# The 64-wide attention stage with its q, k, v and score products as three products of float16 parts

## The reference, cut to what matters

```
b, n, _ = x.shape                       # x is layer-normalised before
q = einsum('bnd,ed->bne', x, Wq).reshape(b, n, H, DH).transpose(0, 2, 1, 3)   # the same for k, v
q = _l2norm(q) * q_scale                # per head, over its 64 channels
k = _l2norm(k) * k_scale
attn = softmax(einsum('bhid,bhjd->bhij', q, k) * DH ** (-0.5))
out = einsum('bhij,bhjd->bhid', attn, v).transpose(0, 2, 1, 3).reshape(b, n, H * DH)
return einsum('bne,de->bnd', out, Wo) + bo
```

## Time and profile before

| | |
|---|---|
| median of 3 runs | 5605.33 us (5605.23 to 5605.4) |
| profiled execution, span | 5817.8 us, 93955 instructions; no other time of it is given |
| busy over the span | PE 4867.1 us (84%), DVE 3629.7 (62%), ACT 3333.5 (57%), POOL 1360.1 (23%) |
| mean granted clock of TensorE | 0.916 |
| this stage, within the span | 3660 to 5435 us |

### The profile page before, as it was taken

One profiled execution on the slowest core, in us unless ns is written; L12 is line 12 of the kernel. 1 busy time (PEld: TensorE's weight loads), 2 busy tenths in 40 slices (PEclk: granted clock), 3 DMA queues, 4 the chain that ended last, 5 costly groups with the idle time before them and its releaser, 6 DMA issues. The chain is left out here.

```text
span 5817.8 us, 93955 instructions
## 1 busy us (share of the span) xinstructions
PE 4867.1 (84%) x29648; PEld 2462.7 (42%) x29648; DVE 3629.7 (62%) x7303; ACT 3333.5 (57%) x5317; POOL 1360.1 (23%) x1406
## 2 busy tenths in 40 slices
PE   6999768559989967868888659799999999999578
PEld 2222268524444436842222246344344344344255
DVE  5344453477777775347777761576776776776750
ACT  6999644425555544447888722555665665655422
POOL 1111045424334405532323045000000000000055
PEclk8999879869999988989999876899999999999777
DMA  3222121213333312132323232200000000000222
GB/s 83 65 65 63 42 56 39 62 57 91 87 94 91 88 49 60 40 92 51 66 50 66 56 67 43 48 1 0 0 0 0 0 0 0 0 0 0 70 43 40
DMA packets 228016, 265.41 MB, mean 46 GB/s; under 512 B 36874, under 2 KB 194410, under 8 KB 221352
## 3 DMA queue, kind: packets, MB, share of 16 engines
q1 hardware_dynamic: 184180, 194.46, 12.6%
q0 software_dynamic: 43520, 66.97, 6.4%
HBM read 163.86 MB, written 96.65 MB: 45 GB/s over the span
## 5 line engine op out<-in xcount | busy, mean ns | idle before, releaser
L3968 ACT ACTIVATE prob_wide<-slot_wide 128x1024 f32<-128x1024 f32 x512 | 497.2, 1026 | 181.9 <-PE slot_wide L3856 181.9
L2184 ACT ACTIVATE prob_decay<-slot_decay 128x640 f32<-128x640 f32 x512 | 358.8, 705 | 343.8 <-PE slot_decay L2031 342.5
L1000 ACT ACTIVATE prob_rms<-slot_rms 128x1024 f32<-128x1024 f32 x512 | 503.9, 1090 | 56.5 <-PE slot_rms L834 54.0
L2518 DVE TENSOR_TENSOR slot_decay<-slot_decay,dtab_decay 128x512 f32<-128x512 f32 (+3 forms) x1024 | 454.1, 494 | 130.0 <-PE slot_decay L2010 109.9
L1000 ACT ACTIVATE prob_relative<-slot_relative 128x1024 f32<-128x1024 f32 x512 | 497.8, 1049 | 42.1 <-PE slot_relative L834 40.6
L3856 PE MATMUL slot_wide<-qT_wide,kT_wide 64*128 64x512 f32 x2048 | 509.5, 616 | 8.0 <-ACT prob_wide L3968 8.0
L3300 POOL DMA_INDIRECT xg_choice_b<-xn_rows_choice_b,ids_choice_b x64 | 61.1, 955 | 1910.1 <-DVE ids_choice_b L3570 1891.5
L3870 PE MATMUL obank_wide<-prob_wide,v_wide 128*64 128x512 f32 x2048 | 467.7, 598 | 15.3 <-issue 11.6
L1373 DVE TENSOR_TENSOR prob_relative<-prob_relative,rtab_relative 128x1024 f32<-128x1024 f32 (+1 forms) x256 | 394.9, 1548 | 134.9 <-ACT prob_relative L1000 126.7
L3944 ACT ACTIVATE rinv_wide<-rbank_wide 128x512 f32<-128x512 f32 x128 | 76.4, 597 | 481.2 <-PE rbank_wide L3881 481.2
L4038 DVE TENSOR_TENSOR sums_wide<-sums_wide,prob_wide 128x1024 f32<-128x1024 f32 x256 | 312.8, 1222 | 15.0
(11 more groups left out here) (861 smaller groups left out, 10385.7 us busy)
## 6 DMA issues: line engine op xcount, KB each, us to landing
scratch_decay<-parts_decay SPq DMA_DIRECT2D x192, 128.0 KB, 2.4
qst_decay<-scratch_decay SPq DMA_DIRECT2D x128, 128.0 KB
scratch_rms<-parts_rms SPq DMA_DIRECT2D x96, 128.0 KB
kst_rms<-scratch_rms POOLq DMA_DIRECT2D x96, 128.0 KB, 5.5
kst_decay<-scratch_decay SPq DMA_DIRECT2D x192, 64.0 KB
kin_decay<-scratch_decay SPq DMA_DIRECT2D x192, 64.0 KB
scratch_relative<-parts_relative SPq DMA_DIRECT2D x96, 128.0 KB
kst_relative<-scratch_relative POOLq DMA_DIRECT2D x96, 128.0 KB, 6.2
```

The costliest lines, as they stand in the source:

```text
L1000: nc.scalar.activation(prob[:, Q % 2, p:G:2, at:at + m], slot[:, u % 3].rearrange("p (k c) -> p k c", k=2)[:, :, 0:m], ACT.Exp).then_inc(e ...
L2184: nc.scalar.activation(prob[:, Q % 2, j, 0:c1 - c0], slot[:, u % 3, c0:c1], ACT.Exp).then_inc(exp_done, 1)
L2518: last = nc.vector.tensor_tensor(sl, sl, dtab[:, h, 0:m], ALU.mult)
L3968: nc.scalar.activation(prob[:, Q % 2, u % 4, :], slot[:, u % 2, :], ACT.Exp).then_inc(exp_done, 1)
```

## The change

The products for q, k, v and the scores are no longer made from float32 operands. Each operand is kept as two float16 tensors, a high part (the value rounded) and a low part (what is left), and a product is the sum of three: high by low, low by high, high by high, added up in PSUM. So that the parts keep their precision, operands are scaled first: Wq and Wk per head by their largest element, Wv per output channel, the LayerNorm output by 2^11, q by 2^14, k by its factor over the largest product of the scales. The scales are undone in the instructions that read the products: ACT's copy and square of q and k, the exponential (a factor per partition), and the factor in Z. The floor of the norm becomes a tensor, `least`. The high parts are written by ACT, the low parts by DVE (one read of PSUM, times the scale, minus the high part); a bank of `bench` is free when the low part is made. In the setup DVE finds the largest elements and scales the weights, and two further loads bring the q and k scales to all partitions.

```diff
+    HALF_MAX = 2.0 ** 14
+    X_SCALE = 2.0 ** 11
+    QK_SCALE = 1.0 / (X_SCALE * HALF_MAX)
+    TINY = 1e-30
+    PRODUCTS = ((1, 0), (0, 1), (0, 0))
...
-        wT = sb("wT", [P, 3, H * W])
+        wT = sb("wT", [P, 2, 3, H * W], F16)
...
-        xnT = sb("xnT", [P, S])
+        xnT = sb("xnT", [P, 2, S], F16)
...
-        kT = sb("kT", [P, C, S])
-        qT = sb("qT", [P, C, S])
+        kT = sb("kT", [P, 2, C, S], F16)
+        qT = sb("qT", [P, 2, C, S], F16)
...
-                 (scales[:, 1, :], A[w["ks"]].rearrange("(c a) o d -> c (a o d)", a=2)), (bo_t[:], rows(A[w["bo"]]))]
+                 (scales[:, 1, :], A[w["ks"]].rearrange("(c a) o d -> c (a o d)", a=2)), (bo_t[:], rows(A[w["bo"]])),
+                 (all_scales[0], rows(A[w["qs"]].rearrange("h o d -> (h o d)"))),
+                 (all_scales[1], rows(A[w["ks"]].rearrange("h o d -> (h o d)")))]
...
                 def turn_weights(n):
+                    if n % 2 == 0 and n < 4:
+                        pe.wait_ge(heads_scaled, n // 2 + 1)
+                    if n == 4:
+                        pe.wait_ge(v_scaled, 1)
...
-                    user[n % 2] = (setup_act, n + 1)
+                    user[n % 2] = (w_low, n + 1) if n < 6 else (setup_act, n - 5)
...
-                        if at_start(b, -1) and t == 0 and half == 0:
-                            pe.wait_ge(setup_act, 4)
+                        if at_start(b, -1) and t == 0:
+                            pe.wait_ge(w_low, 2 * half + 2)
...
-                            nc.tensor.matmul(qk_bank(b, 4 * t + j), xnT[:, t * P:(t + 1) * P],
-                                             wT[:, j // 2, (j % 2) * S:(j % 2 + 1) * S],
-                                             start=True, stop=True).then_inc(qk_filled, 1)
+                            for k, (wp, xp) in enumerate(PRODUCTS):
+                                last = nc.tensor.matmul(qk_bank(b, 4 * t + j), xnT[:, xp, t * P:(t + 1) * P],
+                                                        wT[:, wp, j // 2, (j % 2) * S:(j % 2 + 1) * S],
+                                                        start=(k == 0), stop=(k == len(PRODUCTS) - 1),
+                                                        skip_group_check=True)
+                            last.then_inc(qk_filled, 1)
...
+                        pe.wait_ge(heads_scaled, 2)
...
-                            nc.tensor.matmul(bench[:, j, :], xnT[:, t * P:(t + 1) * P],
-                                             wT[:, 2, j * S:(j + 1) * S], start=True, stop=True).then_inc(v_filled, 1)
+                            for k, (wp, xp) in enumerate(PRODUCTS):
+                                last = nc.tensor.matmul(bench[:, j, :], xnT[:, xp, t * P:(t + 1) * P],
+                                                        wT[:, wp, 2, j * S:(j + 1) * S],
+                                                        start=(k == 0), stop=(k == len(PRODUCTS) - 1),
+                                                        skip_group_check=True)
+                            last.then_inc(v_filled, 1)
...
-                        for hh in range(2):
-                            r = slice(W * hh, W * hh + W)
-                            last = nc.tensor.matmul(slot[:, u % 2, hh * S:(hh + 1) * S], kT[r, Q, kb * P:(kb + 1) * P],
-                                                    qT[r, Q, :], start=True, stop=True)
+                        for i, (kp, qp) in enumerate(PRODUCTS):
+                            for hh in range(2):
+                                r = slice(W * hh, W * hh + W)
+                                last = nc.tensor.matmul(
+                                    slot[:, u % 2, hh * S:(hh + 1) * S], kT[r, kp, Q, kb * P:(kb + 1) * P],
+                                    qT[r, qp, Q, :], start=(i == 0), stop=(i == len(PRODUCTS) - 1),
+                                    skip_group_check=True)
                         last.then_inc(s_filled, 1)
...
+                pe.wait_ge(heads_turned, 1)
+                nc.tensor.transpose(rbank[0:2 * C, 0:P], largest[:, 2, 0:2 * C], ident[:]).then_inc(setup_pe, 1)
+                pe.wait_ge(heads_turned, 2)
+                nc.tensor.transpose(obank[:, 0:2 * C], spread[:], ident[0:2 * C, 0:2 * C]).then_inc(setup_pe, 1)
+                nc.tensor.matmul(rbank[:, P:P + 2 * H], allones[:], one_row[:].rearrange("r c a -> r (c a)"),
+                                 start=True, stop=True, skip_group_check=True).then_inc(setup_pe, 1)
...
+                    act.wait_ge(setup_pe, n + 4)
+                    if n < 6:
+                        nc.scalar.copy(weight_part(n, 0), bench[:, n % 2, :]).then_inc(w_high, 1)
+                    else:
+                        nc.scalar.copy(out_part(n), bench[:, n % 2, :]).then_inc(setup_act, 1)
...
-                        nc.scalar.copy(xnT[:], bench[:, 0, :]).then_inc(xT_ready, 1)
+                        nc.scalar.activation(xnT[:, 0, :], bench[:, 0, :], ACT.Copy, scale=X_SCALE).then_inc(x_high, 1)
...
-                            nc.scalar.copy(qk[:, t, i, half], qk_bank(b, 4 * t + j)).then_inc(qk_drained, 1)
+                            nc.scalar.activation(qk[:, t, i, half], qk_bank(b, 4 * t + j), ACT.Copy, scale=QK_SCALE
+                                                 ).then_inc(qk_drained, 1)
...
-                            nc.scalar.activation(sq[:, i, half], qk_bank(b, 4 * t + j), ACT.Square
+                            nc.scalar.activation(sq[:, i, half], qk_bank(b, 4 * t + j), ACT.Square, scale=QK_SCALE
                                                  ).then_inc(squared, 1)
...
-                        act.wait_ge(setup_pe, C + 1)
-                        nc.scalar.copy(kw[:], obank[:, 0:C]).then_inc(setup_act, 1)
-                        act.wait_ge(setup_act, C + 1)
+                        act.wait_ge(setup_pe, C + 4)
+                        act.wait_ge(setup_dve, 2)
+                        nc.scalar.activation(kw[:], obank[:, 0:C], ACT.Copy, scale=kinv[:, 0:1]).then_inc(setup_act, 1)
+                        act.wait_ge(setup_act, 3)
...
+                        act.wait_ge(turn_filled, m * (2 * C) + (2 * c + 1))
+                        nc.scalar.activation(qT[:, 0, c, :], bench[:, 0, :], ACT.Copy, scale=HALF_MAX
+                                             ).then_inc(q_high, 1)
                         act.wait_ge(turn_filled, m * (2 * C) + (2 * c + 2))
-                        nc.scalar.activation(kT[:, c, :], bench[:, 1, :], ACT.Copy, scale=kw[:, c:c + 1]
-                                             ).then_inc(k_turned, 1)
+                        nc.scalar.activation(kT[:, 0, c, :], bench[:, 1, :], ACT.Copy, scale=kw[:, c:c + 1]
+                                             ).then_inc(k_high, 1)
...
-                        nc.scalar.activation(prob[:, Q % 2, u % 4, :], slot[:, u % 2, :], ACT.Exp).then_inc(exp_done, 1)
+                        nc.scalar.activation(prob[:, Q % 2, u % 4, :], slot[:, u % 2, :], ACT.Exp, scale=peak[:, 1:2]
+                                             ).then_inc(exp_done, 1)
...
+                def largest_of(i):
+                    at = slice(i * C, (i + 1) * C)
+                    link(nc.vector.reduce_max(largest[:, 0, at], scale_part(i), AX_X))
+                    link(nc.vector.tensor_reduce(out=largest[:, 1, at], in_=scale_part(i), op=ALU.min, axis=AX_X))
+                    return nc.vector.scalar_tensor_tensor(out=largest[:, 2, at], in0=largest[:, 1, at], scalar=-1.0,
+                                                          in1=largest[:, 0, at], op0=ALU.mult, op1=ALU.max)
+
+                def scale_heads():
+                    dve.wait_ge(first_loaded, 16 * len(first_loads))
+                    link(largest_of(0))
+                    largest_of(1).then_inc(heads_turned, 1)
+                    dve.wait_ge(setup_pe, 1)
+                    link(nc.vector.reduce_max(by_head[:, 0, :], rbank[0:2 * C, 0:P].rearrange("c (a d) -> c a d", d=W),
+                                              AX_X))
+                    link(nc.vector.tensor_scalar(by_head[:, 0, :], by_head[:, 0, :], TINY, None, ALU.max))
+                    link(nc.vector.reciprocal(by_head[:, 1, :], by_head[:, 0, :]))
+                    nc.vector.tensor_tensor(one_row[:], by_head[:, 1, :].unsqueeze(1).to_broadcast([2 * C, 2 * C, 2]),
+                                            ident[0:2 * C, 0:2 * C].unsqueeze(2).to_broadcast([2 * C, 2 * C, 2]), ALU.mult)
+                    nc.vector.tensor_scalar(spread[:].rearrange("c (a d) -> c a d", d=W),
+                                            by_head[:, 1, :].unsqueeze(2).to_broadcast([2 * C, 2, W]), HALF_MAX, None,
+                                            ALU.mult).then_inc(heads_turned, 1)
+                    dve.wait_ge(setup_pe, 2)
+                    for i in range(2):
+                        nc.vector.tensor_tensor(scale_part(i), scale_part(i), obank[:, i * C:(i + 1) * C].unsqueeze(2)
```

(63 more changed lines are left out.)

33 lines of the change are left out of this document (22 added, 11 removed).

## The result

After the change the kernel takes 5643.9 us (5641.5 to 5645.4, four runs) against 5605.3 us before: ratio 1.0072, 95% interval 1.0058 to 1.0086, so 38.7 us more. In the profiled executions this stage, from the start of its first LayerNorm statistics to the start of its last addition to X, went from 1771.3 to 1813.6 us.

The account below looks back on a forecast made before the run. It took PE to set the pace up to PV(1) and DVE from Z(1) to pair 4's sums; +29 us setup, -7 for the last batch and 14 x (0.15 + 0.5) made +31, so 5636 us, range 5597 to 5682.

Parts of the forecast that it names:

- The bound: Middle batch: PE sets the pace up to PV(1), then DVE works 35.98 us unbroken from Z(1) to pair 4's sums.
- (a): PV(0) to PV(1): four steps, each 0.51 us shorter, bring PV(1) at 17.8 us instead of 19.84, Z(1) at 23.65.
- (b): Z(1) to R(4): DVE's 35.98 us stay untouched; R(4) comes at 59.7 instead of 61.7, a gain of 2.04 us.
- (c): Turns after R(4): a three-turn period takes 11.8 us instead of 11.35; twice per batch, 0.9 us more.
- another time than 0.69 us: Sign of being wrong: a DVE subtraction in the turns that takes a time other than 0.69 us.
- (d): Seventh turn to next PV(0): DVE's chain through LayerNorm statistics and v copies takes 24.3 us instead of 23.0, 1.3 more.
- The clock: PE's idle pieces lower its clock, partly showing in Q0 or the output product: 0.5 us per batch, between 0 and 1.7.
- Setup and ends: Before the first batch: 24.6 us to the first turn, 0.5 and 4.2 in turns, +29 together; batch without successor -7.
- the clock's rival: The clock falls in every batch, in two places or more: 14 x (1.2 to 3) us, 5645 to 5685; chance 0.2.
- PE is the bound throughout: Rival, whole batch: PE's savings all count, 16 x 14.3 us less the setup, giving 5405 us; chance 0.02.
- the weight loads are not hidden: Rival, PE's steps: 1.96 us a step keeps PE's stretches as long as before, 5660 to 5690 us; chance 0.07.
- The handoffs hide: Rival, turns and Q0: (c) and (d) vanish, each batch keeps its 2.04 us, giving 5597 or 5588 us; chance 0.22.

Follow-up runs that it names:

- four_products: Changed kernel with a fourth product, low part by low part, in every q, k, v and score product; +92.4 us against before, ratio 1.0167.
- two_sums_after: Changed kernel without one of DVE's three additions over each pair's probabilities, leaving one block of keys out of the sums; 5591.1 us, 0.9979 of before.
- exp_immediate: Changed kernel with the exponential's factor as a constant in the instruction instead of a value per partition; +36.3 us against before, ratio 1.007.
- v_on_act_after: Changed kernel with both halves of each v block copied by ACT, none by DVE; 5593.3 us, 0.9983 of before.
- fixed_scales: Changed kernel with constants for the searched scales, no weight scaling on DVE and no two further loads; +21.6 us against before, ratio 1.0043.
- scores_parts: Kernel before with only the score products made from parts; q, k and v products stay float32; +37.4 us against before, ratio 1.0065.

## Why the prediction was right, point by point

**The bound.** Right, and shown from both sides: 12 us more of PE per batch cost 2.4 to 4.0 (four_products), 1.23 us less of DVE per pair gave 2.6 to 4.2 (two_sums_after), most of it in DVE's run.

**(a), (b).** A step of 1.40 us and PV(1) at 17.91 us after PV(0) (said: 17.8). DVE's run began at 23.77 and took 36.2 us (said: 23.65 and 35.98); R(4) came at 60.00 us instead of 61.72, said 59.7. The 0.3 us of difference are Z's factor per partition (0.75 instead of 0.69 us, three times in the run) and the exponential's (0.14 us, by exp_immediate), both priced at nothing. The waits of PE come out otherwise than said: 2.83 us ahead of PV(4) (said 3.4), and none ahead of R(4) in this batch, because PV(4) itself is slower.

**(c).** From R(4) to the seventh turn it is 24.84 us (4548.17 - 4523.33) where 23.70 stood (R(4) 61.72 us after PV(0), and that PV(0) at 4481.18, so 4566.60 - 4542.90): +1.14, said +0.9. Two three-turn periods took 11.82 and 12.01 us. The k subtraction takes 0.74 us, not 0.69; the prediction had named another time than 0.69 us as a sign of being wrong. That sign came, though the forecast held.

**(d).** From the seventh turn to PV(0) 24.45 us instead of 23.0: +1.45, said +1.3, and DVE turned from the sums of pair 7 to the LayerNorm statistics 9.20 us behind the turn, as counted. The waits for v copies stand where the prediction put them. v_on_act_after shows that the lengthening reaches PV(0) through these copies in DVE's list: without them PV(7) to PV(0) is 15.36 us, 1.76 us shorter than before the change.

**The clock.** Here a term was wrong: 0.5 us per batch "in Q0, or into the output product". The clock falls at PV(4) instead, in ten of batches 1 to 14, where it is covered by the wait ahead of R(4), as the prediction had said of that place; PEclk is 1.00 in the last stretch of the batch shown.

The Trainium skill (TensorE: Matmul & The Clock Gate, section HAM oscillation) tells of a kernel in which the waits between bursts bring the engine back to half rate every time. The 5.35 us rows agree that it happens; the 3.27 us wait in exp_immediate, behind which PV(4) took 3.65 us in eleven of fourteen batches, shows that here it does not happen every time. What decides it in one batch and not in the next was not found.

**Per batch** the two errors offset: 0.89 us (109.31 - 108.42) against 0.15 + 0.5. The clock's 0.5 us did not come, and the rest was under-sized by 0.74: 0.3 in (a) and (b), 0.24 in (c), 0.15 in (d). That the batch came within 0.24 us of the forecast is luck.

**Setup and ends.** First statistics to PV(0) of batch 0: +32.0 us, said +29. To the first turn +25.1 (said 24.6), in the first two turns +1.7 (said 0.5), and in the six turns, which lie 2.41 us apart and not 2.2, +5.4 (said 4.2). There PE works in single turns between waits, and the windows of the kernel after show the clock low:

```profile
3571.00:3580.00 9.00, 6.87 (x31) 4.86 (x32) 5.11 (x8) 4.37 (x7) 0.00 (x0) 0.64 0.00 0
```

The search and scaling are worth 17 of it by the medians and 19.2 by the traces, shown by fixed_scales; that the two loads cost nothing is consistent with it, but no run took them alone. The savings at the end were over-sized: -2.8 and -1.0 us against -3.9 and -3.1. In the last batch a pair takes 8.63 us after the change and 8.79 before, and 8.45 in exp_immediate, so half of what a pair was to gain went to the exponential's 0.10 us. The first interval (batch 0 to 1) lost 2.6 us and not 0.65. In its last stretch the clock does fall: PEclk is 0.79 from 3690.00 to 3698.20 us, a score step takes 2.72 us, and the stretch takes 20.26 us where the middle batches have 19.05. The rest of it was not followed.

**The sum** of the profiled stage is 32.0 + 2.6 + 13 x 0.89 - 2.8 - 1.0 = +42.3 us, said +31; the medians differ by 38.7, and the interval of the ratio puts the difference between 33 and 48 us, so the 3.6 us between these two can't be told from nothing. The forecast was low by 11 us against the traces: 3 in the setup, 2 in the first interval, 3 in the middle batches and 3 at the end.

The profiled execution of after spans 5639.6 us and not the 5849 us that the prediction gives. It had taken the 212 us by which the profiled execution of before exceeds its median for something that carries over. They did not lie in this stage: outside it the profiled execution of before takes 4046.5 us and that of after 3826.0.

**The rivals.** The upper end of the clock's rival, 5685, does not follow from its own terms: 14 x 3 us above the sum without clock is 5671. "PE is the bound throughout" and "the weight loads are not hidden" fell with the steps of 1.40 us and four_products. "The clock in two or more places" fell for this kernel, but two_sums_after shows the mechanism where the wait is on the path. "The handoffs hide" fell with the three-turn periods of 11.82 and 12.01 us where 11.35 stood, and with scores_parts, in which a batch is 1.88 us longer.
